# Passes 3 and 4 of a five-pass graph network: GpSimd waits, behind every four row gathers, until the first three have landed

## The reference

```python
x = layernorm(x + L0(x, ...))   # edge MLP on [x[src], edge_attr], mean over dst, node MLP
x = layernorm(x + L1(x, ...))   # degree-scaled sum of x[src] over dst, GCN, residual, batch norm
x = layernorm(x + L2(x, ...))   # mean of x[src] over dst, linear, elu
x = layernorm(x + L3(x, ...))   # two relational convolutions, below

def _rgcn_conv(x, src, dst, edge_type, edge_weight, W, root, bias):
    xj = x[src]
    m = sum over r of (edge_type == r) * (xj @ W[r])
    m = m * edge_weight[:, None]
    return segment_sum(m, dst) + x @ root + bias
```

## Time and profile before

| | us |
|---|---|
| median of 3 runs without the profiler | 3856.42 (3853.22 to 3861.42) |
| span of the profiled execution | 4761.8 |
| profiled pass 0, first gather to last | 1344.2 |
| profiled passes 1 and 2 | 761.9 |
| profiled pass 3 | 1201.2 |
| profiled pass 4 | 1186.2 |

### The profile page before, as it was taken

The page is one execution under the profiler, slowest core; times in us unless marked ns, Lnnn a source line. Parts: engine busy times, 40 slices in busy tenths (PEclk is TensorE's granted clock), DMA queues, the critical chain, the costliest instruction groups (busy, mean ns, idle before and its releaser), DMA issues.

```text
span 4761.8 us, 69331 instructions
## 1 busy us (share of the span) xinstructions
PE 3833.3 (81%) x23096; PEld 3228.5 (68%) x23096; DVE 2287.6 (48%) x7830; ACT 2017.5 (42%) x4824; POOL 2652.2 (56%) x2744
## 2 busy tenths in 40 slices
PE   5888888888888997899577778777766777777777
PEld 4777777777776886788466666555555666766666
DVE  5777777777676555666434334333321222222222
ACT  3444434444445554565444444444443333433332
POOL 5666666566542654555565565555656556564554
PEclk7999998998899998999788888888887788888878
DMA  6555555555555664666234333333333334443333
GB/s 197 151 147 149 152 149 150 148 148 149 144 151 145 149 152 105 160 172 165 89 127 137 128 134 131 125 116 127 127 114 105 118 113 124 128 125 112 121 115 97
DMA packets 438618, 642.39 MB, mean 135 GB/s; under 512 B 266274, under 2 KB 310818, under 8 KB 438115
## 3 DMA queue, kind: packets, MB, share of 16 engines
q1 hardware_dynamic: 310162, 375.66, 25.2%
q0 software_dynamic: 100880, 235.32, 18.7%
q10 hardware_dynamic: 27202, 26.78, 1.8%
HBM read 468.80 MB, written 168.73 MB: 134 GB/s over the span
## 4 chain that ended last, share of the span: by engine, by line
PE 28%; another core or an unknown queue 10%; issue 8%; DVE 5%; ACT 1%; DVEq 0%; DMA 0%; POOL 0%; ACTq 0%; POOLq 0%; SPq 0%
PE bank L1715 9%; PE bank L1654 6%; PE bank L1679 4%; PE bank L1700 3%; PE bank L1690 3%; PE bank L1645 1%; DVE w_both L1489 1%; DVE work L1557 1%; DVE work L1489 1%; DVE late_lo L1537 1%; PE bank L2353 0%; PE bank L2370 0%; DVE work L1582 0%; ACT work L2665 0%
## 5 line engine op out<-in xcount | busy, mean ns | idle before, releaser
L652 POOL DMA_INDIRECT work<-table_rel,reli x1462 | 1385.7, 948 | 1060.0 <-issue 426.4
L652 POOL DMA_INDIRECT work<-table_pre,srci x831 | 816.7, 983 | 537.6 <-issue 237.3
L2660 ACT ACTIVATE work<-iota,local 128x72 f32<-128x72 f32 x1464 | 378.4, 344 | 609.1 <-remote 346.8
L1034 ACT ACTIVATE X<-bank 128x468 uint8<-128x468 f32 (+1 forms) x624 | 323.9, 545 | 708.7 <-PE bank L976 375.1
L1654 PE MATMUL bank<-work 128*128 128x72 f32 x2928 | 425.0, 290 | 245.9 <-issue 234.8
L1654 PEld LDWEIGHTS bank<-work 128*128 128x128 f32 x2928 | 417.4, 212 | 265.5 <-issue 242.5
L2665 ACT ACTIVATE work<-work,ew,src_both 128x72 f32<-128x72 f32 x1464 | 515.4, 436 | 15.7 <-remote 9.7
L937 PE MATMUL bank<-w_both,work 128*128 128x256 f32 x1664 | 473.2, 409 | 33.3 <-issue 14.5
L1406 PE MATMUL bank<-counts,piece_hi 128*128 128x468 f32 x1176 | 464.7, 395 | 28.4 <-issue 12.9
L1406 PE MATMUL bank<-counts,piece_lo 128*128 128x468 f32 x1176 | 450.2, 383 | 0.0
L949 PE MATMUL bank<-work 128*128 128x64 f32 x3328 | 423.0, 281 | 22.3 <-issue 21.4
(11 more groups left out here) (326 smaller groups left out, 6489.9 us busy)
## 6 DMA issues: line engine op xcount, KB each, us to landing
work<-ea_cols SPq DMA_DIRECT2D x208, 256.0 KB
kept<-work SPq DMA_DIRECT2D x50, 880.0 KB
kept<-w_both SPq DMA_DIRECT2D x50, 880.0 KB
work<-kept SPq DMA_DIRECT2D x50, 880.0 KB
w_both<-kept SPq DMA_DIRECT2D x50, 880.0 KB
adj<-X SPq DMA_DIRECT2D x156, 225.0 KB
work<-adj SPq DMA_DIRECT2D x60, 585.0 KB
work<-table_rel,reli POOLq DMA_INDIRECT x1462
```

The lines of the kernel that those rows point to most:

```text
L652: pool.indirect_dma_start(into[:, u, :], None, tables[p], bass.IndirectOffsetOnAxis(ap=idx_of(p)[:, t:t + 1].bitcast(U32), axis=0)).then_i ...
L1034: act.activation(stage[:, j % A_STAGES, lo * AW:hi * AW], bank[A_BANKS_AT[b % 2]][:, 0:(hi - lo) * AW], ACT.Copy).then_inc(a_taken, 1)
L2660: ins = act.activation(hot3[:, u, :], iota[:, 0:PAIR_WIN], ACT.Abs, bias=local[:, t:t + 1], scale=-1.0)
```

## The change

Each group of four gathers in passes 3 and 4 is split: the first three add to `late_gathered[n % 4]` as before, the fourth adds to `late_ended[n % 4]`. `late_ended` is a new name for four semaphores that pass 0 used (`gathered[4..7]`), so their counts go on from where pass 0 left them. Behind each group of four, GpSimd waits until the first three of it have landed, and then goes on; only behind the last pair of a pass it does not. TensorE waits for both semaphores ahead of a pair's matmuls. There are 2 x 93 = 186 such waits in pass 3 and 2 x 88 = 176 in pass 4, 362 in all.

```diff
-        late_gathered = sems("late_gathered", LATE)
+        late_gathered, late_ended = sems("late_gathered", LATE), gathered[SLOTS0 - LATE:]
...
-        def fetch(pool, p, g, into, landed, skipped=0):
-            for u in range(U - skipped):
+        def fetch(pool, p, g, into, landed, skipped=0, first=0, last=U):
+            for u in range(first, min(last, U - skipped)):
...
                 for o in range(2):
-                    fetch(pool, p, 2 * h + o, late_gat[n % LATE][:, o * U:(o + 1) * U, :], late_gathered[n % LATE],
-                          padded(2 * h + o))
-
-
-        def late_padded(n):
-            lasts = (len(G_PAIRS) - 1, len(G_PAIRS) + len(L_PAIRS[1]) - 1)
-            return sum(PADDED for m in lasts if m <= n and m % LATE == n % LATE)
+                    to = late_gat[n % LATE][:, o * U:(o + 1) * U, :]
+                    fetch(pool, p, 2 * h + o, to, late_gathered[n % LATE], padded(2 * h + o), 0, U - 1)
+                    fetch(pool, p, 2 * h + o, to, late_ended[n % LATE], padded(2 * h + o), U - 1)
+                    if n < (len(G_PAIRS), len(G_PAIRS) + len(L_PAIRS[1]))[p - 3] - 1:
+                        pool.wait_ge(late_gathered[n % LATE], late_landed(n)[0] - (1 - o) * (U - 1) * 16)
+                        pool.sem_inc(gate, 1)
+
+        def late_landed(n):
+            lasts = [m for m in (len(G_PAIRS) - 1, len(G_PAIRS) + len(L_PAIRS[1]) - 1) if m <= n and m % LATE == n % LATE]
+            more = min(PADDED, 1) * len(lasts)
+            rest = PADDED * len(lasts) - more
+            pass0 = GROUPS // SLOTS0 * U - (PADDED if n % LATE == LATE - 1 else 0)
+            return (n // LATE + 1) * (PU - 2) * 16 - rest * 16, (n // LATE + 1) * 2 * 16 - more * 16 + pass0 * 16
...
-                    pe.wait_ge(late_gathered[n % LATE], (n // LATE + 1) * 16 * PU - late_padded(n) * 16)
+                    pe.wait_ge(late_gathered[n % LATE], late_landed(n)[0])
+                    pe.wait_ge(late_ended[n % LATE], late_landed(n)[1])
```

## The result

| | before | changed |
|---|---|---|
| median without the profiler, us | 3855.5 | 4373.6 |
| ratio, 95% interval | | 1.134 (1.1324 to 1.1356) |
| span of the profiled execution, us | 4761.8 | 4371.7 |

The change costs 518 us, 1.43 us for each of its 362 pauses. The profile shown of the kernel before is 905 us longer than its timed runs; the changed kernel's is as long as its timed runs (the profiled execution is one of the four, 4373.5 us with a span of 4371.7). So the two profiles, set side by side, say "390 us faster", and the timed runs say 518 us slower.

The account below looks back on a forecast made before the run. The prediction took GpSimd's row of gathers to bound passes 0, 3 and 4, with TensorE just behind or level. 3856 + 253 for pauses - 26 hidden = 4083 us, 5.9% slower; range 3740 to 4190.

Parts of the forecast that it names:

- The bound: Passes 0, 3 and 4: GpSimd's row of gathers, 1.25 us apart, is the path; floor 3830 to 3897 us.
- The gathers and TensorE's extra wait at nothing: Passes 3 and 4: same gathers on another semaphore cost nothing; TensorE's 183 extra waits cost 0, or 18 us if uncovered.
- The price of a pause: GpSimd's wait behind each group of four: 0.70 us in the mean, 253 us over 362, bounds 105 and 576.
- The quiet pause: A GpSimd wait with no other transfer near: 2.2 landing plus 0.79 restart less 2.50, so 0.49 us.
- The disturbed pause: A GpSimd wait that meets an 880 KB piece or table store: landing at most 3.30 us, so 1.59 us.
- The share of disturbed pauses: Passes 3 and 4: one pause in five meets a large transfer, with DMA engines busy 0.38 of the time.
- What hides it: GpSimd's idle time in the timed runs absorbs part of the pauses: 26 us by the lower floor.
- The profiled execution: Its 905 us above the timed median are waits absent without the profiler; changed profiled span level or shorter, 4500 to 4760.
- The hold is real: Rival: gathers in a row hold TensorE's releases without the profiler too, so pauses gain; 3717 us, up to 3840; chance 0.24.
- TensorE hides the pauses: Rival: TensorE bounds passes 3 and 4, so the pauses change nothing; 3856 us, within 8; chance 0.09.
- The pause is dearer: Rival: every GpSimd pause in passes 3 and 4 costs 1.59 us, 4406 us in all; chance 0.03.

Follow-up runs that it names:

- The second profile of before: The kernel before, unchanged, profiled once more: 3857.4 us, with a span of 3855.5 us.
- the thin kernel: Changed kernel with its 880 KB stores and loads cut to their first 16 columns: 4209.1 us; the kernel before with the same cut: 3860.3 us.
- the series of one to four landings: Changed kernel with GpSimd waiting for the first one, two, three or all four gathers of each group: 3903.4, 4102.6, 4373.6, 4759.9 us.

## Why the prediction was wrong in its size

**The bound: right.** The floor of 3830 to 3897 us from GpSimd's pace was no coincidence. The second profile of before has no GpSimd wait on TensorE in passes 3 and 4 beyond the usual gap, and a gather left out gives 1.246 us.

**The gathers and TensorE's extra wait at nothing: right** (3856.3 us with the split alone).

**The price of a pause: the step that failed.** The forecast took 0.70 us, between bounds of 0.29 and 1.59; it is 1.43, of which 1.37 stand at the pauses and 0.06 in the late starts inside groups, for which the forecast had no term. Three parts of the term were too small:

- The quiet pause, put at 0.49 us, is 0.86 in the timeline and 0.90 in the mean of the thin kernel. The landing was right (2.2 us, also in the kernel that waits for all four). The restart of 0.79 us was read from a release by TensorE, counted from the end of a matmul; from a gather's last packet to the next gather it is 1.1 us. That is 0.3 us, 362 times, about 110 us.
- The disturbed pause, put at 1.59 us as an upper bound, is 2.25 us in the row shown. In the changed kernel's trace 102 pauses cost more than 1.59 us, up to 4.5. The bound from the earlier trace rows came from one gather beside whatever transfers ran then; it was not an upper bound of anything.
- The share of disturbed pauses, put at one in five, is nearly twice that. Counted in the trace, 134 of the 362 pauses (0.37) cost more than 1.2 us, 2.25 in the mean, and the other 228 cost 0.86. Counted by traffic instead, 127 stretches from the awaited gather's start to the next group's first hold over 100 packets of other queues; these cost 2.22 us in the mean, the other 235 cost 0.92. The share was guessed from a busy share of the DMA engines averaged over the pass.

Put into the forecast's own sum, the counted terms give 362 x (0.63 x 0.86 + 0.37 x 2.25), about 498 us; with the 21.6 us of late starts inside groups that is the whole loss. This only adds up what the trace holds. What shows the cause is the series of one to four landings and the thin kernels.

**What hides it: wrong, and small.** The forecast granted 26 us of idle time. The second profile of before has none inside the two passes.

**The profiled execution: wrong.** The forecast put the 905 us of difference down to the profiler, and from that said that the profiled span would come out at 4500 to 4760 us; it is 4371.7. The profile of before caught a disturbed execution, in which TensorE's releases came late behind the gathers; none of the thirteen further profiles showed it, the changed kernel's included. The argument that the held releases are not in the timed runs, which decided the sign, was right whatever their cause. By the page quoted with it, the Trainium skill (Runtime: NRT & Kernel Launch, The ~15µs preamble/postamble breakdown), the profile's total stands about 6.2 us above the reported time. The span used here, from the first to the last instruction, stands 1.9 us below the time of the same execution (4371.7 and 4373.5 us, 3855.5 and 3857.4): the size and the sign are not the page's, but the two do lie close together. So a gap of 905 us should have been read as "this execution is not like the timed ones". What held TensorE in it stays open. That it was the profiler's records, for which the forecast named the Trainium skill (NOTIFIC — the notification-queue block, Interfaces), no run here supports.

**The rivals.** "The hold is real" is refuted by the timed runs and by the second profile. "TensorE hides the pauses" is refuted by the kernel with fewer gathers. "The pause is dearer", at 4406 us, comes nearest and was given 0.03. Its nearness is in part luck: it priced every pause at 1.59 us, where most cost 0.86 and over a third 2.25. The range was cut below it, at 4190, and that cut is the mistake in the range: 1.59 us was an end of an unknown cost, and nothing in the rows excluded it.

## What to carry to other kernels

Before pausing an engine to relieve another, work out how much idle time that engine has in the timed runs: count its instructions times its pace and set the sum against the median. If it fills the time, a wait costs the whole chain from the awaited start to the restart, less what is issued meanwhile. Where a profile is far longer than the timed runs, its waits are not those of the timed runs; take another profile, or trust only paces and durations in it. And for a cost that no row shows, let the range reach both ends of it.

## What the runs showed of the hardware that was not expected

- From a gather's last packet to the start of a gather that waited for it 1.1 us pass (1.09 in the median of the quiet waits for all four), so the start-to-start chain through a landing is 3.36 us for 128 rows of 512 bytes, though the gather's own row shows only 0.94 us. The Trainium skill (DMA: Bandwidth & Descriptors, Anatomy of one DMA — SWDGE (gpsimd) path) gives about 2.0 us of fixed cost plus the bytes for one such DMA, with some 50 ns for dispatch; the trace agrees for the landing (2.2 us), but whoever prices a wait with 2.2 us misses a third of the chain.
- Transfers of 880 KB cost a stream of gathers nothing while nobody waits for a single landing (3860.3 us with them cut, 3859.5 with them whole), and 164 us as soon as somebody does.
- 362 waits that are already met cost nothing measurable on GpSimd's queue, between DMAs 1.25 us apart.
